# Attention scores of a banded and a causal core as four products of 32 columns

## What is computed

```
# first layer, banded
scores = jnp.einsum('bhnqd,bhnkd->bhnqk', qb, kb) * scale
scores = jnp.where(allowed, scores, NEG)          # allowed: 0 < dist <= 128
attn = jax.nn.softmax(scores, axis=-1)
out = jnp.einsum('bhnqk,bhnkd->bhnqd', attn, vb)
...
# third layer, causal; q_dir and k_dir are q and k over their norms
scores = jnp.einsum('bhnd,bhmd->bhnm', q_dir, k_dir)
scores = scores * (r_q * sq) * (jnp.swapaxes(r_k, -2, -1) * sk)
scores = jnp.where(mask, scores, -jnp.inf)        # mask: lower triangle
out = jnp.einsum('bhnm,bhmd->bhnd', jax.nn.softmax(scores, axis=-1), v)
```

## Time and profile before

| what | us |
|---|---|
| median of 3 runs | 2809.06 (2807.59 to 2812.19) |
| profiled execution, its own time | 2799.33 |
| its span, first to last instruction | 2797.6 |
| TensorE busy, products | 2356.6 (84%) |
| VectorE busy | 1851.0 (66%) |
| ScalarE busy | 1566.4 (56%) |
| GpSimd busy | 630.0 (23%) |

### The profile page before, as it was taken

The page is one execution under the profiler, slowest core; times in us unless marked ns, Lnnn a source line. Parts: engine busy times, 40 slices in busy tenths (PEclk is TensorE's granted clock), DMA queues, the critical chain, the costliest instruction groups (busy, mean ns, idle before and its releaser), DMA issues. The chain is left out here.

```text
span 2797.6 us, 50742 instructions
## 1 busy us (share of the span) xinstructions
PE 2356.6 (84%) x18701; PEld 1161.5 (42%) x18746; DVE 1851.0 (66%) x2753; ACT 1566.4 (56%) x3173; POOL 630.0 (23%) x1194
## 2 busy tenths in 40 slices
PE   5985566799999999779996999999688877876778
PEld 2543343133333333247763333333346645644633
DVE  5644766999999999131225777777295476557577
ACT  2542452488888888633333577767457447633321
POOL 3860000000000000000001112122185166303356
PEclk8986777699999999989996899999898998987789
DMA  3310002321112111000002222221100010010000
GB/s 92 80 45 0 11 1 84 79 51 50 30 48 51 44 34 28 5 3 1 1 1 74 62 67 66 60 74 29 35 24 23 1 34 4 2 29 3 1 0 16
DMA packets 62320, 93.87 MB, mean 34 GB/s; under 512 B 25299, under 2 KB 37749, under 8 KB 62074
## 3 DMA queue, kind: packets, MB, share of 16 engines
q1 hardware_dynamic: 54330, 86.02, 11.7%
q10 hardware_dynamic: 7744, 4.59, 0.8%
HBM read 75.87 MB, written 10.49 MB: 31 GB/s over the span
## 5 line engine op out<-in xcount | busy, mean ns | idle before, releaser
L938 DVE TENSOR_REDUCE l1a_core_mpart<-l1a_core_psA 128x1 f32<-128x1024 f32 x512 | 600.9, 1219 | 41.1 <-PE l1a_core_psA L850 29.5
L920 ACT ACTIVATE l1a_core_prob<-l1a_core_psB 128x512 f32<-128x512 f32 x1024 | 552.0, 596 | 98.8 <-PE l1a_core_psB L865 79.6
L1280 ACT ACTIVATE l2a_core_prob<-l2a_core_psB 128x384 f32<-128x384 f32 (+3 forms) x656 | 303.9, 526 | 154.6 <-PE l2a_core_psB L1218 149.0
L1305 DVE TENSOR_REDUCE l2a_core_mpart<-l2a_core_psA 128x1 f32<-128x1024 f32 (+4 forms) x352 | 292.1, 879 | 57.5 <-PE l2a_core_psA L1202 56.1
L877 PE MATMUL l1a_core_psV<-l1a_core_prob,l1a_core_vh 128*32 128x512 f32 x2048 | 265.5, 594 | 0.2 <-ACT l1a_core_prob L920 0.2
L865 PE MATMUL l1a_core_psB<-l1a_core_qh,l1a_core_kh 75*32 75x512 bf16 x2560 | 195.5, 381 | 0.8 <-ACT l1a_core_prob L920 0.8
L1234 PE MATMUL l2a_core_psV<-l2a_core_prob,l2a_core_vh 128*32 128x256 f32 (+3 forms) x1856 | 174.9, 431 | 0.5
L2135 DVE SCALAR_TENSOR_TENSOR X<-l1e_psO,W,X 128x128 f32<-128x128 f32 x128 | 36.0, 345 | 197.0 <-PE l1e_psO L2083 197.0
L2118 ACT ACTIVATE l1e_h<-l1e_psH,l1e_w_b 128x512 f32<-128x512 f32 x128 | 87.8, 687 | 137.3 <-PE l1e_psH L2076 137.1
L1147 POOL TENSOR_SCALAR_AFFINE_SELECT l2a_core_prob<-l2a_core_prob 128x128 f32<-128x128 f32 x256 | 73.9, 292 | 335.2 <-ACT l2a_core_prob L1280 331.3
L2083 PEld LDWEIGHTS l1e_psO<-l1e_w_w,l1e_h 128*128 128x128 f32 x1024 | 118.7, 192 | 13.4 <-issue 13.4
(11 more groups left out here) (677 smaller groups left out, 4435.4 us busy)
## 6 DMA issues: line engine op xcount, KB each, us to landing
l2f_tab<-in_rotary SPq DMA_DIRECT2D x32, 128.0 KB, 2.1
l0a_core_qh<-qparts SPq DMA_DIRECT2D x36, 96.0 KB
l0a_core_kh<-kparts SPq DMA_DIRECT2D x36, 96.0 KB
l1a_core_qa<-qparts SPq DMA_DIRECT2D x32, 96.0 KB
l1a_core_ka<-kparts SPq DMA_DIRECT2D x32, 96.0 KB
l2a_core_qa<-qparts SPq DMA_DIRECT2D x32, 96.0 KB
l2a_core_ka<-kparts SPq DMA_DIRECT2D x32, 96.0 KB
l1a_core_qh<-qparts SPq DMA_DIRECT2D x30, 96.0 KB
```

The costliest lines, as they stand in the source:

```text
L920: nc.scalar.activation(prob[u % (2 * PER_KB)][:], psB[u % 3][:], ACT.Exp, scale=scale).then_inc(b_exped, 1)
L938: nc.vector.tensor_reduce(mpart[:, n // 2, n % 2:n % 2 + 1], psA[i % 2][:], AX.X, ALU.max).then_inc(a_freed, 1)
L1280: nc.scalar.activation(prob[n % RING][:, 0:cols], psB[n % 3][:, 0:cols], ACT.Exp, scale=scale).then_inc(b_exped, 1)
L1305: ins = nc.vector.tensor_reduce(mpart[:, place, part:part + 1], psA[i % 2][:, lo * P:hi * P], AX.X, ALU.max)
```

## The change

The second scores of the causal core and first scores, mask and second scores of the banded core are issued as four products each. Each of the four has 32 columns of the weights and writes 32 partitions of the same PSUM columns. Moving operand, sums and order stay as they were, as do the semaphores: the last of the products counts up. The causal core's first scores, its diagonal slots and both transposes of the maxima are not touched.

```diff
--- before.py
+++ after.py
@@ -586,13 +586,18 @@
                     if h:
                         pe.wait_ge(qk_loaded[b], 96 * (h // BUFS + (b > 0)))
                 for e in range(2):
-                    mm(ps[:, e * CH:(e + 1) * CH], g.identb[:], (g.window_q if n + e else g.window_q0)[:], start=True,
-                       stop=False, skip_group_check=True)
+                    for j in range(COL_TILES):
+                        cols = slice(j * COLS, (j + 1) * COLS)
+                        mm(ps[cols, e * CH:(e + 1) * CH], g.identb[:, cols], (g.window_q if n + e else g.window_q0)[:], start=True,
+                           stop=False, skip_group_check=True)
                 for i in range(4):
                     qb = 4 * n + i
                     oldest = max(qb - 1, 0)
-                    ins = mm(ps[:, (2 * i + 2) * P - (qb + 1 - oldest) * P:(2 * i + 2) * P], qh[b][0:QK_ROWS, qb * P:(qb + 1) * P],
-                             kh[b][0:QK_ROWS, oldest * P:(qb + 1) * P], start=False, stop=True, skip_group_check=True)
+                    for j in range(COL_TILES):
+                        lo = qb * P + j * COLS
+                        ins = mm(ps[j * COLS:(j + 1) * COLS, (2 * i + 2) * P - (qb + 1 - oldest) * P:(2 * i + 2) * P],
+                                 qh[b][0:QK_ROWS, lo:lo + COLS], kh[b][0:QK_ROWS, oldest * P:(qb + 1) * P], start=False,
+                                 stop=True, skip_group_check=True)
                 ins.then_inc(a_scored, 1)
 
             def score(h, u):
@@ -605,8 +610,10 @@
                     pe.wait_ge(b_exped, n - 2)
                 for i, kb in enumerate(key_blocks(u)):
                     cols = min(2, NT - kb) * P
-                    ins = mm(psB[n % 3][:, 2 * i * P:2 * i * P + cols], kh[b][0:QKM_ROWS, kb * P:(kb + 1) * P],
-                             qh[b][0:QKM_ROWS, kb * P:kb * P + cols], start=True, stop=True, skip_group_check=True)
+                    for j in range(COL_TILES):
+                        lo = kb * P + j * COLS
+                        ins = mm(psB[n % 3][j * COLS:(j + 1) * COLS, 2 * i * P:2 * i * P + cols], kh[b][0:QKM_ROWS, lo:lo + COLS],
+                                 qh[b][0:QKM_ROWS, kb * P:kb * P + cols], start=True, stop=True, skip_group_check=True)
                 ins.then_inc(b_scored, 1)
 
             def values(h, j):
@@ -1214,9 +1221,11 @@
                     pe.wait_ge(b_exped, n - 2)
                 q4 = qh[h % 3][0:QKM_ROWS, :].rearrange("p (c n) -> p c n", c=NC)
                 for at, kb, c, low, groups in b_units[u]:
-                    out = psB[n % 3][:, at * P:(at + groups * (4 - low)) * P]
-                    ins = mm(out.rearrange("p (c n) -> p c n", c=groups), kh[h % 3][0:QKM_ROWS, kb * P:(kb + 1) * P],
-                             q4[:, c:c + groups, low * P:CH], start=True, stop=True, skip_group_check=True)
+                    for j in range(COL_TILES):
+                        lo = kb * P + j * COLS
+                        out = psB[n % 3][j * COLS:(j + 1) * COLS, at * P:(at + groups * (4 - low)) * P]
+                        ins = mm(out.rearrange("p (c n) -> p c n", c=groups), kh[h % 3][0:QKM_ROWS, lo:lo + COLS],
+                                 q4[:, c:c + groups, low * P:CH], start=True, stop=True, skip_group_check=True)
                 ins.then_inc(b_scored, 1)
 
             def values(h, kb):
```

## The result

The changed kernel takes 2780.93 us (2769.87 to 2786.96, 5 runs) against 2809.06 us for the kernel before (2799.61 to 2815.53, 5 runs): ratio 0.9894, 95% interval 0.986 to 0.9929, 28 us faster. The forecast was 2786 us, within 2769 to 2802. The profiled execution took 2780.93 us, its span 2779.2 us.

The account below looks back on a forecast made before the run. The prediction took TensorE to bound both cores, with borders between array shapes as most of its non-column time. Banded -7 and causal -16 us sum to -23, from 2809 to 2786 us; 8 in 10 range 2769 to 2802.

Parts of the forecast that it names:

- The border's price: TensorE in both cores: each border where the array's shape changes costs 0.10 to 0.11 us; 75x32 beside 128x32 costs nothing.
- 0 for the weight loads: Both cores: four loads of 32 columns for one of 128 cost nothing extra, by the run of 14 value products.
- the mark set in the prediction: Sign of being wrong: a group of four 256-column products takes over 0.11 us.
- The causal core: Causal core's term: 322 borders go, 33.8 us x 0.6, less 4.4 us for new borders, -16 us.
- The factor 0.6: Causal core: 0.4 of the 33.8 us from removed borders is lost to waits on VectorE's maxima, 0.6 comes through.
- The new borders: Causal core: 44 borders beside 128-wide diagonal slots and transposes, 0.10 us each, cost 4.4 us.
- The banded core: Banded core's term: heads go from 8.16 to 7.63 us, some 14 heads in the steady state, -7 us.
- five borders a head: Banded core: five borders of 0.105 us vanish with effect, 0.53 us a head.
- Issue of instructions: Rival, 8%: banded core's 398 instructions a head become the bound, deciding from 20.5 ns each; about 2839 us.
- The gaps without a releaser: Sign of being wrong: pauses inside the banded core for which the profile shows no releaser.
- VectorE takes nearly all: Rival, 12%: two thirds and more of the causal gain waited away, GpSimd holds banded values; some 2801 us.
- nothing waits: Rival, 12%: borders go without new waits, full 29 us in the causal core, 9 in the banded; about 2770 us.

Follow-up runs that it names:

- half maxima: Causal core's partial maxima taken over half of each piece's columns: in the kernel before 2787.73 us (0.9916), in the changed kernel 2752.52 us (0.9806), both against the kernel before.

## Why the prediction was right, point by point

**The border's price** held: overlaps of 0.17 were forecast between scores and values, 0.18 to 0.21 were seen, and with 64 columns the pauses came back. That 75x32 and 128x32 count as the same division of the array was read off the wide core, and it carried over. So did 0 for the weight loads, taken by the nearer row: 0.11 us for a group of four, the mark set in the prediction.

**The causal core** was -16 and came out at -23 with -19 in the steady order. The factor 0.6 for what VectorE lets through was 0.68: 4.8 us saved in four heads and 1.1 us of new borders, over 41 x 0.21 = 8.6 us. The half maxima show that VectorE is most of what held the rest, as the waits of the earlier trace rows had been read. Some 3 us more are the clock's, which the prediction allowed for with 1 to 3 us and left out of the sum. The new borders cost what the sum had for them: 1.1 us in four heads on paper, 1.2 us won when they were taken out.

**The banded core** was -7 and measured -6.5, but the step didn't hold: five borders a head were to give 7.63 us, and in the changed kernel a head averages 7.94. The missing term is SyncE's queue: 12 issues a head, 7.87 us end to end. The prediction didn't add up the queue's issues, though each of them has its row in the trace of the kernel before. It named GpSimd as the next limit, at 6.9 us of work a head, and found a little room in 7.63 us. That was its busy time; end to end the same instructions take 7.52 us, so there was hardly any. With three of the issues elsewhere and in time the heads are at 7.53, where GpSimd holds them. What TensorE alone would give isn't shown; it is at least the 0.63 us from 8.16 to 7.53, a little more than the five borders of the sum. That the whole came out at -6.5 all the same is luck in part: the steady heads account for 2 to 3 us, and a higher clock in the last head, which isn't shown to be the change's, for about 2.

**Issue of instructions** (8%) is out. In the changed banded core 2620 products and 2616 loads in the 104 us from 79 to 183 us make 20 ns an instruction, and the heads of 7.53 us with 398 instructions 18.9 ns, below the 20.5 from which it was to decide. The 62 ns or so per product that the Trainium skill gives in "TensorE: Matmul & The Clock Gate", section "Wait — 56ns, not 53.3ns?", for hardware decode off doesn't apply to this kernel: those 104 us make 40 ns a product. The gaps without a releaser inside the banded core, a sign of being wrong in the prediction, were SyncE's and not those of issue.

**VectorE takes nearly all** (12%) and **nothing waits** (12%) are both out: the causal core's 19 to 23 us lie between the 16 of the forecast and the 29 without waits, and its half maxima show both that VectorE took something and that it took less than half. What the first of the two said of the banded core, that GpSimd holds up the values of a shorter head, came true once SyncE's queue was out of the way.

## What to carry to other kernels

Look at TensorE's order of work for neighbours that divide the array into different columns: here each such border cost 0.10 to 0.11 us, and giving both sides 32 columns removed it at no price in loads or issue. Before forecasting a shorter period, add up each DMA queue's issues per period and compare the sum with the new one: a queue with 0.3 us to spare becomes the next bound. Do the same for an engine that is named as the next limit, by the time from start to start of its instructions where it never waits: GpSimd's 6.9 us of busy time were 7.52 us end to end. When loads move to another queue, work out when their reader needs them and not only how long they take to issue.

## What was not expected of the hardware

*Column groups run on their own.* With 32 columns on both sides, records of scores and values lie between one another, in the changed kernel's banded core:

```profile
114.74 0.27 PE L615 MATMUL l0a_core_psB<-l0a_core_qh,l0a_core_kh 75*32 75x256 bf16 x1
114.76 0.28 PE L631 MATMUL l0a_core_psV<-l0a_core_prob,l0a_core_vh 128*32 128x128 f32 x3
114.85 0.27 PE L615 MATMUL l0a_core_psB<-l0a_core_qh,l0a_core_kh 75*32 75x256 bf16 x1
114.86 0.28 PE L631 MATMUL l0a_core_psV<-l0a_core_prob,l0a_core_vh 128*32 128x128 f32 x3
```

The program has all values of this run ahead of the next scores; the group of columns that has one product fewer, and is done with its values, starts its scores while the others still stream. In the causal core, where values of different lengths stand side by side, scores begin here 0.38 us ahead of the end of the values' record:

```profile
1690.11 1.03 PE L1243 MATMUL l2a_core_psV<-l2a_core_prob,l2a_core_vh 128*32 128x384 f32 x8
1690.76 0.77 PE L1227 MATMUL l2a_core_psB<-l2a_core_qh,l2a_core_kh 75*32 75x512 bf16 x8
```

The sum had an overlap of 0.17 at most. What this adds to the gain I haven't measured apart.

*One transfer can be slower than three.* A key transfer of 288 KB with an outermost dimension of 3 took 0.73 us to issue against 1.4 us for three of 96 KB (3 x 0.46 to 0.48), but had only three packets under way at a time, and the small transfer behind it started 4 to 6 us after its issue.

*The same load costs less to issue elsewhere:* 0.30 us on ScalarE's queue, 0.46 to 0.48 us on SyncE's.
